# Clamped tiles split between VectorE and TensorE, placed from a table, in a sorted-bump attention and MoE kernel

## What is computed

```python
out_i = sum_j max(0, 1 - |z_i - z_j|/b_h) * v_j      # over the keys j of the batch
```

## Time and profile before

| | |
|---|---|
| median of 3 runs | 2274.71 us |
| lowest, highest | 2269.26, 2275.46 us |
| profiled execution, span | 2269.9 us (the page gives no other time for it) |
| PE / DVE / ACT / POOL busy in the span | 2004.6 / 1949.9 / 1928.9 / 972.7 us |
| the loop over 1024 tiles | about 87 to 1889 us of the span |

### The profile page before, as it was taken

The page is one execution under the profiler, slowest core; times in us unless marked ns, Lnnn a source line. Parts: engine busy times, 40 slices in busy tenths (PEclk is TensorE's granted clock), DMA queues, the critical chain, the costliest instruction groups (busy, mean ns, idle before and its releaser), DMA issues.

```text
span 2269.9 us, 30762 instructions
## 1 busy us (share of the span) xinstructions
PE 2004.6 (88%) x11838; PEld 737.5 (32%) x11838; DVE 1949.9 (86%) x2792; ACT 1928.9 (85%) x1284; POOL 972.7 (43%) x412
## 2 busy tenths in 40 slices
PE   6889989988989899987899999768999999899957
PEld 4423223222322232221222222212222224677733
DVE  4699999898999999999999999999999997644428
ACT  3599999999999999999999999999999996122214
POOL 1010010020318539533276376332774574377747
PEclk9999999999999999999999999989999999899989
DMA  6415334524421202131212030312120305698988
GB/s 224 183 42 200 122 113 130 184 92 157 158 111 33 86 22 98 38 116 56 93 33 86 22 114 24 114 65 84 33 86 24 105 3 128 166 244 233 217 221 306
DMA packets 184535, 259.27 MB, mean 114 GB/s; under 512 B 22728, under 2 KB 162632, under 8 KB 176200
## 3 DMA queue, kind: packets, MB, share of 16 engines
q1 hardware_dynamic: 169904, 237.84, 31.4%
q0 software_dynamic: 12288, 18.88, 4.5%
q10 hardware_dynamic: 2200, 0.60, 0.1%
HBM read 187.25 MB, written 70.03 MB: 113 GB/s over the span
## 4 chain that ended last, share of the span: by engine, by line
ACT 50%; PE 17%; DVE 11%; POOL 8%; DMA 7%; issue 6%; SPq 0%; POOLq 0%; DVEq 0%; ACTq 0%
ACT TB L1139 49%; PE ps L931 6%; DVE TB L1466 5%; POOL scr L1647 4%; PE ps L841 4%; DMA y_rows<-ZB 3%; PE ps L878 2%; POOL y_rows L1755 1%; DVE TB L1488 1%; DMA ZB<-zq_rows 1%; PE ps L1040 1%; DVE st L1198 1%; POOL TB L1741 1%; PE ps L986 1%; PE ps L886 1%
## 5 line engine op out<-in xcount | busy, mean ns | idle before, releaser
L1139 ACT ACTIVATE TB<-ZB,nzk 128x2048 f32<-128x2048 f32 x932 | 1776.7, 2042 | 53.6 <-DMA ZB<-zq_rows 47.7
L931 PE MATMUL ps<-TB,V 128*32 128x512 f32 x8192 | 1087.1, 624 | 182.7 <-DVE TB L1466 148.9
L1466 DVE TENSOR_SCALAR TB<-TB 128x2048 f32<-128x2048 f32 x932 | 1109.5, 1219 | 41.6 <-ACT TB L1139 40.2
L1647 POOL TENSOR_TENSOR scr<-ebase,scr 128x256 f32<-128x256 f32 x12 | 517.5, 43125 | 0.0
L931 PEld LDWEIGHTS ps<-TB,V 128*32 128x32 f32 x8192 | 188.4, 110 | 829.9 <-DVE TB L1466 498.1
L878 PE MATMUL ps<-XF,wsgu 128*128 128x512 f32 x512 | 277.0, 634 | 0.0
L1617 POOL TENSOR_SCALAR ve<-mv 128x4 f32<-128x4 f32 x44 | 50.4, 1145 | 520.1 <-DVE mv L1202 519.9
L1488 DVE SCALAR_TENSOR_TENSOR TB<-ZB,kz 128x2048 f32<-128x2048 f32 x92 | 216.6, 2354 | 0.0
L1645 POOL TENSOR_TENSOR scr<-ebase,scr 128x4 f32<-128x4 f32 x12 | 42.4, 3530 | 353.5 <-DVE scr L1332 353.5
L1171 ACT ACTIVATE ZB<-ps 128x128 f32<-128x128 f32 x64 | 17.7, 277 | 170.5 <-PE ps L1017 117.5
L878 PEld LDWEIGHTS ps<-XF,wsgu 128*128 128x128 f32 x512 | 81.9, 190 | 170.7 <-issue 169.4
(11 more groups left out here) (196 smaller groups left out, 1747.7 us busy)
## 6 DMA issues: line engine op xcount, KB each, us to landing
ZB<-zq_rows SPq DMA_DIRECT2D x64, 1024.0 KB, 7.0
scr<-fused_w SPq DMA_DIRECT2D x32, 512.0 KB, 3.5
TB<-y_rows SPq DMA_DIRECT2D x24, 512.0 KB, 8.0
TB<-in_egu_w SPq DMA_DIRECT2D x44, 256.0 KB
y_rows<-zero SPq DMA_DIRECT2D x20, 512.0 KB, 5.0
fused_w<-TB SPq DMA_DIRECT2D x4, 2048.0 KB, 14.5
scr<-fused_w SPq DMA_DIRECT2D x32, 256.0 KB, 2.7
XF<-in_x SPq DMA_DIRECT2D x24, 256.0 KB, 5.8
```

The costliest lines, as they stand in the source:

```text
L931: ins = pe.matmul(ps[k][32 * c:32 * c + 32, :], V[:, o:o + 32], tile(n)[:, 512 * c:512 * c + 512], start=(kb == 0), stop=(kb == KB - 1))
L1139: act.activation(tile(e), zrow(head), ACT.Abs, bias=nzk[b][:, kb * H + g:kb * H + g + 1], scale=1.0).then_inc(s_abs, 1)
L1466: dve.tensor_scalar(T, T, 1.0, 1.0, ALU.min, ALU.subtract).then_inc(s_bump, 1)
L1647: pool.tensor_tensor(E4[:, :, 0:64], view(ebase[:, 0:1], 0, [[0, 4], [0, 64]]), E4[:, :, 0:64], ALU.pow).then_inc(s_ex, 1)
```

## The change

Three things. **Clamps:** an own tile no longer needs |z_i − z_j|. DVE writes two tiles from the query row, clamp(z, u, u+1) (kind "c") and clamp(z, u−1, u) (kind "m"), each one tensor_scalar with max and min and two per-partition columns. Their difference is min(|z − u|, 1). PE multiplies the first by V and the second by a negated V, so an own tile is now two entries of the ring and two PE steps. The "− 1" is missing in them; its effect, the sum of V over the own key blocks, is made on PE by a matmul with ones (unit "S", once per quad, into `Sq`) and subtracted in `vector_quad_scale`. The key columns and the negated V are made on GpSimd per quad (`pool_keys`), in one of two halves of `held`; DVE and PE wait for them (`s_own`). `kz` and `vector_columns` go.

**Table:** 140 own tiles instead of 92, placed by a string per quad: "a" is a pair of usual tiles of two neighbouring heads, "c" an own tile. They are 6, 8, 6, 6 in the quads of batch 0 and 8, 10, 10, 10 in each later batch; before they were 3, 8, 5, 4, then 5, 6, 7, 6, and 5, 7, 6, 6 twice. They lie in the first three (or last three) key blocks of a quad.

**Staggered pairs:** heads 0 and 1 of a quad run 3 pairs ahead of heads 2 and 3. Copies of heads 0 and 1 now stand 4 and 2 entries before the quad's end, those of heads 2 and 3 at entries 2 and 4 of the next; transposes 2 before the end and at 0, 2, 4. The `timetable` shifts too: `rest_at` 51 + 49k, `hn` one slot later, query rows loaded at 57, 58, 62, 63. Between a "c" and its "m" nothing advances but the own slot: an "m" entry has the place of the entry behind it.

```diff
-def own_tiles():
-
-
-    own, ahead = set(), 0
-    for b in range(NB):
-        _, dv, ac, _ = timetable(b)
-        beside = [0] * (SLOTS + 1)
-        for e in dv:
-            beside[min(e[0], SLOTS)] += WEIGHTS[e[1]]
-        for e in ac:
-            beside[min(e[0], SLOTS)] -= 5
-        for n in range(SLOTS):
-            q, i = 4 * b + n // 64, n % 64
-            ahead += 7 - beside[n] - (7 if i in (63, 0, 4) else 11 if i == 3 else 4 if i in (6, 9, 12) else 0)
-            if ahead > 15 and 4 <= i < 60:
-                own.add(256 * b + n)
-                ahead -= 43
-            ahead = max(ahead, -60)
-    return own
+           "rm": 15, "re": 8, "sc": 14, "sm": 5, "sg": 4, "gu": 7, "dn": 4, "S": 2}
+
+PARTS = {"S": 1, "xT": 1, "hT": 1, "mT": 1, "zT": 1, "v": 2, "z": 32, "lg": 4, "gu": 2, "dn": 2}
+
+
+LAG = 3
+PLACES = [
+    "acacaaaacaaaaaaaaacaaaaaaaccaaaaaaa",
...
+    "acaaaaaccaaacaacaacaacaaaaaacccaaaaaa",
...
+def filled(q, order, clamps):
+
+
+    rows = (clamps + 3) // 4
+    kbs = list(range(KB - rows, KB)) if q % 4 == 3 else list(range(rows))
+    own = [(kb, j) for kb in kbs for j in range(4)]
+    own = own[:clamps]
+    first = [("a", kb, 0) for kb in range(KB) if (kb, 0) not in own]
+    second = [("a", kb, 2) for kb in range(KB) if (kb, 2) not in own]
+    tiles = first[:LAG]
+    a_, b_ = first[LAG:], second
+    while a_ or b_:
+        if a_ and len(a_) >= len(b_) - LAG:
+            tiles.append(a_.pop(0))
+        else:
+            tiles.append(b_.pop(0))
+    tiles, cl = iter(tiles), iter(own)
+    return kbs, own, [next(cl if o == "c" else tiles) if o == "a" else ("c",) + next(cl) for o in order]
+
+
+def entries():
+
+
+    o = []
+    for q, (kbs, own, slots) in enumerate(plan()):
+        for kind, kb, j in slots:
+            if kind == "a":
+                o += [(q, "a", kb, j), (q, "a", kb, j + 1)]
+            else:
+                o += [(q, "c", kb, j), (q, "m", kb, j)]
+    return o
...
 def rest_at(blk):
-    return 52 + 48 * blk
+    return 51 + 49 * blk
...
+    for i in range(4):
+        pe += [(64 * i + 10, ("S", 4 * b + i))]
+        dv += [(64 * i + 18, "S", 4 * b + i)]
...
-            dv += [(r, "xst", p, k, 0), (r + 1, "xst", p, k, 1), (r + 5, "hn", p, k, 0), (r + 6, "hn", p, k, 1),
+            dv += [(r, "xst", p, k, 0), (r + 1, "xst", p, k, 1), (r + 6, "hn", p, k, 0), (r + 7, "hn", p, k, 1),
-            s = 64 * ((n - NZB) % H // 4) + 61 + (n - NZB) % 4
+            s = 64 * ((n - NZB) % H // 4) + (57, 58, 62, 63)[n % 4 - 2]
...
+            if what == "S":
+                kbs, own, _ = quads[b]
+                for kb in kbs:
+                    o, w = kb * C + 64 * (b % 4), 16 * sum(h == kb for h, _ in own)
+                    ins = pe.matmul(out_[:, 0:w], view(one[:, 0:1], 0, [[0, 128]]), V[:, o:o + w], start=(kb == kbs[0]),
+                                    stop=(kb == kbs[-1]))
+                ins.then_inc(full[bank], 1)
...
-            pe.wait_ge(s_bump, n + 1)
-            if kb == 0 and m:
+            if kind == "m":
+                pe.wait_ge(s_own, q + 1)
+            pe.wait_ge(s_bump, bump_by[e])
+            if first_of[q, j] == e and m:
                 pe.wait_ge(empty[k], m)
             o = kb * C + (4 * (q % 4) + j) * D
+            w = view(negated(q, quads[q][0].index(kb)), D * j, [[1, 32]]) if kind == "m" else V[:, o:o + 32]
             for c in range(4):
-                ins = pe.matmul(ps[k][32 * c:32 * c + 32, :], V[:, o:o + 32], tile(n)[:, 512 * c:512 * c + 512],
-                                start=(kb == 0), stop=(kb == KB - 1))
-            ins.then_inc(full[k] if kb == KB - 1 else s_used, 1)
+                ins = pe.matmul(ps[k][32 * c:32 * c + 32, :], w, tile(e)[:, 512 * c:512 * c + 512],
+                                start=(first_of[q, j] == e), stop=(last_of[q, j] == e))
+            ins.then_inc(full[k] if last_of[q, j] == e else s_used, 1)
...
-                for n in range(SLOTS):
-                    q, i = 4 * b + n // 64, n % 64
-                    if q and i in (0, 3, 6, 9):
-                        tensor_quad_out(q - 1, i // 3)
-                    for e in pace.due(n):
+                for n in range(begin[4 * b], begin[4 * b + 4]):
+                    q = E[n][0]
+                    i, rest = n - begin[q], begin[q + 1] - n
+                    if rest == 2 and q < 15:
+                        tensor_quad_out(q, 0)
+                    if q and i in (0, 2, 4):
+                        tensor_quad_out(q - 1, i // 2 + 1)
+                    if b and n == begin[4 * b]:
+                        pe.wait_ge(q_vl[0], 128 * b)
+                    for e in pace.due(place(n)):
                         tensor_stage(*e)
-                    if b and n in (0, 32):
-                        pe.wait_ge(q_vl[n // 32], 128 * b)
-                    tensor_step(256 * b + n)
+                    if b and n == upper[b]:
+                        pe.wait_ge(q_vl[1], 128 * b)
+                    tensor_step(n)
...
-            dve.tensor_copy(view(ctxn[:, 0, 0:1], 64 * (q % 4) + 16 * t, [[C, 4], [4 * C, 4], [1, 16]]),
-                            view(ps[bank][:, 0:1], 0, [[128, 4], [32, 4], [1, 16]])).then_inc(empty[bank], 1)
+            dve.tensor_tensor(view(ctxn[:, 0, 0:1], 64 * (q % 4) + 16 * t, [[C, 4], [4 * C, 4], [1, 16]]),
+                              view(ps[bank][:, 0:1], 0, [[128, 4], [32, 4], [1, 16]]),
+                              view(Sq[q % 2][:, 0:1], 16 * t, [[0, 4], [0, 4], [1, 16]]), ALU.subtract).then_inc(empty[bank], 1)
...
-                vector_columns(b)
-                for n in range(SLOTS):
-                    q = 4 * b + n // 64
-                    if q and n % 64 in (3, 6, 9, 12):
-                        vector_quad_scale(q - 1, n % 64 // 3 - 1)
-                    if q < 15 and n % 64 == 63:
-                        vector_quad_copy(q, 0)
-                    elif q and n % 64 in (0, 3, 4):
-                        vector_quad_copy(q - 1, (0, 3, 4).index(n % 64) + 1)
-                    for e in pace.due(n):
+                dve.wait_ge(s_nz, b + 1)
+                for n in range(begin[4 * b], begin[4 * b + 4]):
+                    q, kind, kb, j = E[n]
+                    i, rest = n - begin[q], begin[q + 1] - n
+                    if q < 15 and rest in (4, 2):
+                        vector_quad_copy(q, 2 - rest // 2)
+                    if q and i in (2, 4):
+                        vector_quad_copy(q - 1, i // 2 + 1)
+                    if q and i in (0, 2, 4, 6):
+                        vector_quad_scale(q - 1, i // 2)
+                    for e in pace.due(place(n)):
                         vector_stage(v, *e)
-                    if 256 * b + n + 1 in own and n + 1 < SLOTS:
-                        vector_distances(b, n + 1)
-                    T = tile(256 * b + n)
-                    dve.wait_ge(*distances(256 * b + n))
-                    if 256 * b + n in own:
-                        o = n // 4 % 16 * H + 4 * (q % 4) + n % 4
-                        top = kz[:, 1, o:o + 1]
-                        dve.tensor_scalar(T, T, top, top, ALU.min, ALU.subtract).then_inc(s_bump, 1)
+                    if kind != "a":
+                        vector_clamp(n)
                     else:
-                        dve.tensor_scalar(T, T, 1.0, 1.0, ALU.min, ALU.subtract).then_inc(s_bump, 1)
+                        dve.wait_ge(s_abs, abs_by[n])
+                        dve.tensor_scalar(tile(n), tile(n), 1.0, 1.0, ALU.min, ALU.subtract).then_inc(s_bump, 1)
...
+        def vector_clamp(e):
+
+            q, kind, kb, j = E[e]
+            head = 4 * q + j
+            i = 4 * quads[q][0].index(kb) + j
+            if kind == "c":
+                dve.wait_ge(s_own, q + 1)
+                dve.wait_ge(q_zb[head % NZB], 16 * (head // NZB + 1))
...
-            dve.scalar_tensor_tensor(tile(e), zrow(head), kz[:, 0, kb * H + g:kb * H + g + 1], zrow(head), ALU.subtract, ALU.max,
-                                     reverse0=True).then_inc(s_dist, 1)
+            low = 1 if kind == "c" else 0
+            dve.tensor_scalar(tile(e), zrow(head), key_column(q, low, i), key_column(q, low + 1, i),
+                              ALU.max, ALU.min).then_inc(s_bump, 1)
...
                 if b:
                     for k in range(4):
                         pool_minus(k, 4 * (b - 1) + k, p, 1e-5 * NT * NT)
+                    pool_keys(4 * b + 1)
                     for k in range(4):
                         pool_rstd(k, s_xmv, 4 * (b - 1) + k + 1, s_xrs, p)
                         if k:
                             pool_weights(b - 1, k - 1)
                         pool_route(b - 1, k)
+                        if k != 2:
+                            pool_keys(4 * b + (2, 3, 0, 4)[k])
                     pool_weights(b - 1, 3)
                 else:
                     for n in range(4, 4 * NB):
                         pool_rstd(n % 4, s_fmv, n + 1, s_frs, p)
```

(91 more changed lines are left out.)

74 lines of the change are left out of this document (40 added, 34 removed).

## The result

The changed kernel takes **2262.1 us** (median of 13 runs, 2260.4 to 2267.6) against 2271.8 for the kernel before in the same runs: ratio 0.9963, 95% interval 0.9953 to 0.9972. A second set of 12 runs gave 2263.1 against 2269.3, ratio 0.9976 (0.9964 to 0.9988). So 6 to 9 us are gained, 0.2 to 0.4%, where I forecast 32.5 (1.4%). The time lies inside my range of 2196 to 2272, but the gain is under a third of the forecast. My starting point, the median of 3 runs (2274.7), was 3 us above that of the 13.

What follows compares the result with a forecast made beforehand. Three full engines, ACT, DVE and PE, were taken to bound the loop, each part falling to its fullest engine's need: −11 − 10.5 − 15 + 4 = −32.5 us off 2274.7 gives 2242 us, range 2196 to 2272.

Steps and rivals of the forecast that it cites:

- Batch 0: ACT, 442, −11: Batch 0 of the loop: comes down to ACT's need of 442 us from 453, a gain of 11 us.
- Light parts: −3.5 each: The 106 us at each later batch's start: falls to DVE's need, 102.5 us; three times, 10.5 us gained.
- FFN stretches: −5 each: The 344 us with FFN blocks in each later batch: falls to PE's need, 339 us; three times, 15 us gained.
- Rival B: FFN stretches: PE fills up, the ring of 8 can't smooth it, they gain nothing; 2257 us (2248 to 2270), chance 0.18.
- GpSimd: +4: Key sets of 5.0 us ahead of `pool_rstd` delay `hn` at six places; a third of 13 us charged, +4 (0 to 24).
- Rival C: Before `hn`: GpSimd's keys cost 12.1 us, DVE stands 9.2 us at six places, 55 us; 2293 us, chance 0.10.
- D: Clamps on DVE run at the two-input rate, 281 us more on the full DVE; 2523 us, chance 0.02.
- rival A: Whole loop: DVE and PE follow ACT, so all 91 us come; 2184 us (2184 to 2205), chance 0.15.
- Stagger: Quad ends: removes most of DVE's 23.8 and PE's 23.9 us of waits, letting DVE reach its need; not counted separately.

## Why the prediction was wrong

**The failed step is the sum of batch 0 (and of the z parts of batch 1): "Batch 0: ACT, 442, −11".** I priced PE by pitch for the later batches alone. For batch 0 I compared ACT and DVE and left PE out, although shows it busy for 405 of 453 us there. Three stretches of some 45 slots carry 32 z parts each. The window of such a stretch in the kernel before, and PE's timeline in it, before and after:

```profile
355.00:425.00 70.00, 69.04 (x390) 21.59 (x390) 61.22 (x50) 67.68 (x37) 0.00 (x0) 1.00 0.47 155
```

```profile
395.77 1.23 PE L841 MATMUL ps<-scr,XF 128*128 128x512 f32 x2
396.93 1.06 PE L931 MATMUL ps<-TB,V 128*32 128x512 f32 x8
397.93 1.23 PE L841 MATMUL ps<-scr,XF 128*128 128x512 f32 x2
399.09 1.92 PE L931 MATMUL ps<-TB,V 128*32 128x512 f32 x16
400.94 1.23 PE L841 MATMUL ps<-scr,XF 128*128 128x512 f32 x2
```

```profile
400.06 2.09 PE L912 MATMUL ps<-scr,XF 128*128 128x512 f32 x4
402.08 1.07 PE L1005 MATMUL ps<-TB,V 128*32 128x512 f32 x8
402.96 1.04 PE L1005 MATMUL ps<-TB,held 128*32 128x512 f32 x8
403.82 1.04 PE L1005 MATMUL ps<-TB,V 128*32 128x512 f32 x8
404.79 1.23 PE L912 MATMUL ps<-scr,XF 128*128 128x512 f32 x2
```

Before, three slots and two z parts take 5.17 us without a gap, 1.72 a slot: PE was full already (69.0 of 70 us), with ACT just behind (67.7). After, the m step of each own tile adds 0.86 (402.96 to 403.82). At the old spacing of the z parts the three stretches with them, from the first to the last z matmul, take 83.7, 86.5 and 86.1 us before and 88.5, 89.1 and 88.6 with the changed kernel's own tiles (the run with the old spacing).

The first part got 8 us longer (two profiles each) where I had 14.5 shorter, the first light part in it: 23 us missed. Without the m matmuls it takes 540.7 us instead of 556, so PE's m steps, which I had put at nothing here, are 15 to 16 us of the 23. Without the m clamp as well it takes 533.7, about the 533.5 that my forecast comes to: the rest is DVE's. On the complete kernel 12 fewer own tiles give 6 us back, and 17 in the old way 10.

**Light parts: −3.5 each, measured +1.3 to +1.8.** The work was right: between the marks 3 own tiles became 6, 6 × 2.70 − 3 × 3.70 − 3 × 1.19 = +1.5 us, and DVE's busy time rose by 1.6. What failed are the 3 to 4% that I let it gain: DVE was busy for 97% before and for 96% after. No quad end lies between these marks, so the stagger had nothing to give back there.

**FFN stretches: −5 each, measured −11 in all.** Nearly right, and the mechanism too: PE full, clock 1.00, ACT waiting through the ring, DVE close behind. Rival B gave the time that was measured (2248 to 2270, chance 0.18), but not for its reason: it had the FFN stretches gain nothing, and they are what gained. That the time lies in my range is luck: the room that I had left for a miss in the FFN stretches was used up by misses in the other parts.

**GpSimd: +4, measured none.** A key set costs 3 × 0.48 + 2.0 us, 3.4 and not 5.0:

```profile
L1831 POOL TENSOR_SCALAR held<-nzk 128x12 f32<-128x12 f32 x27 | 12.3, 479 | 0.5
L1841 POOL TENSOR_SCALAR held<-V 128x192 f32<-128x192 f32 x9 | 18.0, 2004 | 0.0
```

No wait of DVE for `rs` stands among those of 0.6 us and more in the changed kernel's loop; I had 1 to 4 us at each of six places. Rival C is out; so is D: 1339 ns.

**ACT, rival A**: 2184 needs both PE and DVE out of the way, as the run with neither shows (2186).

**Stagger, the second step that failed**: I said that without the quad-end waits DVE comes down to its need. They did vanish; but waits of DVE for PE's transposes took their place, 29.5 us at L1477 against 5.9 at L1393 before. And the new order, priced by the run with 92 own tiles in the old way, is 31 us slower than the old one where I had it at nothing or better. Clamps and further tiles gave 38 us, and the order took most of them. Through which waits it does so stays open.

## What to carry to other kernels

Price every engine in every stretch, the one that isn't moved as well: here the change shifts ACT's work to PE and DVE, and in each stretch one of these was full. Where two ways to make the same tile load different engines, choose by stretch: the way that is cheap on DVE where DVE is full, the way that is cheap on PE where PE is. When three engines are within a few per cent of each other, taking load from one of them gives back less than its share. And time a new order by itself, with the old work in it, before adding work that is to profit from it.

## What the runs showed that I had not expected

Removing 120 us of PE's pitch gave 37 us, and removing both 120 us of PE's and some 176 us of DVE's gave 76: no single engine's load explains the time. The new order with 92 own tiles made in the old way cost 31. The part behind the loop varies by 8 us between executions of untouched code. And the granted clock was 1.00 in slots 13 to 57 with PE busy for 53.3 of 77 us in the changed kernel, but 0.87 before with 53.3 of 75, and 0.87 again with the m matmuls away and PE busy for 52.9 of 77: part of those two stretches ran at 1.2 GHz, all of the first at 2.4. What beside the busy time decides it, these runs don't settle.
